# Unit-triangular 128x128 inverses by Horner's rule over block columns, and layer norms as (a - mean) * scale

## The reference

```python
x0 = layernorm(x)                       # (x - m) / sqrt(v + eps), no weights
h  = layernorm(x0) * dn_g + dn_b
q, k, v = split(h @ gates_w + gates_b, 3);  lr = h @ lr_w + lr_b
k  = k / norm(k)
A  = tril(k @ k.T, -1) + eye(512)
u  = solve_triangular(A, v, lower=True)
y  = (q @ k.T) @ (lr * u) ;  x1 = x0 + y @ out_w + out_b
x2 = x + x1 + relu((layernorm(x1) * mn_g + mn_b) @ w1 + b1) @ w2 + b2
out = x2 + (silu(n @ wg.T) * (n @ wu.T)) @ wd.T,   n = layernorm(x2)
```

## Time and profile before

| | us |
|---|---|
| Median of 3 runs (range) | 1793.11 (1792.05 to 1793.13) |
| The profiled execution, its own time | 1798.49 |
| Its span in the trace | 1796.8 |
| PE busy | 1713.0 (95%) |
| DVE busy | 1264.6 (70%) |
| POOL busy | 970.2 (54%) |
| ACT busy | 760.8 (42%) |

### The profile page before, as it was taken

How to read it: one execution, slowest core, us unless ns; L and a number is a source line. 1 busy time by engine, 2 the same in 40 slices (tenths; PEclk the granted TensorE clock), 3 DMA queues, 4 the chain that set the end, 5 groups by cost and what they waited for, 6 DMA issues and landing times.

```text
span 1796.8 us, 32849 instructions
## 1 busy us (share of the span) xinstructions
PE 1713.0 (95%) x11682; PEld 1549.5 (86%) x11682; DVE 1264.6 (70%) x2927; ACT 760.8 (42%) x1626; POOL 970.2 (54%) x1269
## 2 busy tenths in 40 slices
PE   5899999579999999999999999999999999999997
PEld 5899999478888889888888888888888899888886
DVE  4677787257777776777777777777776666676664
ACT  4668777123333333333333333333333333333432
POOL 4456775235555555555555555555555555555552
PEclk8999999689999999999999999999999999999999
DMA  4655565311111121111111211111112111111100
GB/s 124 229 194 186 200 209 181 139 40 41 52 53 52 52 76 52 54 59 56 53 53 53 76 52 52 53 52 52 52 53 64 53 51 51 51 53 59 61 16 24
DMA packets 112669, 140.83 MB, mean 78 GB/s; under 512 B 42389, under 2 KB 94872, under 8 KB 112536
## 3 DMA queue, kind: packets, MB, share of 16 engines
q1 hardware_dynamic: 112536, 139.11, 23.5%
HBM read 80.03 MB, written 59.05 MB: 77 GB/s over the span
## 4 chain that ended last, share of the span: by engine, by line
PE 62%; POOL 8%; DVE 6%; issue 4%; ACT 1%; DMA 0%; POOLq 0%; DVEq 0%; ACTq 0%
PE ps L150 29%; PE ps L1002 12%; PE ps L1012 8%; PE ps L917 5%; POOL xn L1447 5%; PE ps L933 4%; PE ps L923 3%; DVE a L1411 2%; POOL sc L1437 2%; DVE bs L1416 1%; POOL ls L1439 1%; DVE mv L1229 1%; DVE hf L1265 1%; ACT sg L1131 1%; POOL sc L1441 0%
## 5 line engine op out<-in xcount | busy, mean ns | idle before, releaser
L1490 POOL TENSOR_TENSOR hl<-hf,hh 128x512 fp32r<-128x512 f32 x128 | 172.6, 1349 | 394.0 <-ACT hh L1136 394.0
L1012 PE MATMUL ps<-wdT,hh 128*128 128x256 f32 x768 | 203.9, 303 | 1.1 <-ACT sg L1131 0.9
L1265 DVE TENSOR_TENSOR hf<-ps,sg 128x512 f32<-128x512 f32 x192 | 132.5, 690 | 88.1 <-PE ps L1002 85.1
L1012 PE MATMUL ps<-wdT,hl 128*128 128x256 f32 x768 | 187.2, 281 | 0.3 <-DVE hl L1270 0.3
L1136 ACT ACTIVATE hh<-hf 128x512 fp32r<-128x512 f32 x192 | 121.4, 632 | 155.1 <-DVE hf L1265 152.0
L1131 ACT ACTIVATE sg<-ps 128x512 f32<-128x512 f32 x192 | 113.6, 592 | 134.3 <-PE ps L1002 134.3
L1002 PE MATMUL ps<-xh3T_hi,wgT 128*128 128x512 f32 x384 | 154.7, 403 | 0.7 <-DVE xh3T_lo L1270 0.7
L1140 ACT ACTIVATE z_hi<-ps 128x256 fp32r<-128x256 f32 x128 | 49.2, 385 | 248.3 <-PE ps L933 246.6
L1002 PE MATMUL ps<-xh3T_lo,wgT 128*128 128x512 f32 x384 | 152.3, 396 | 0.0
L1002 PE MATMUL ps<-xh3T_lo,wuT 128*128 128x512 f32 x384 | 152.0, 396 | 0.0
L1002 PE MATMUL ps<-xh3T_hi,wuT 128*128 128x512 f32 x384 | 151.9, 396 | 0.0
(11 more groups left out here) (223 smaller groups left out, 5818.6 us busy)
## 6 DMA issues: line engine op xcount, KB each, us to landing
gg_scratch<-gg SPq DMA_DIRECT2D x32, 640.0 KB, 3.3
gg<-gg_scratch SPq DMA_DIRECT2D x32, 640.0 KB, 3.8
kx_scratch<-kx SPq DMA_DIRECT2D x32, 522.0 KB, 2.8
kx<-kx_scratch SPq DMA_DIRECT2D x32, 522.0 KB, 3.5
xk<-in_L_attn_x_dram SPq DMA_DIRECT2D x32, 512.0 KB, 4.1
xt<-in_L_attn_x_dram SPq DMA_DIRECT2D x32, 512.0 KB, 4.6
out_dram<-ot SPq DMA_DIRECT2D x32, 512.0 KB, 2.9
low_scratch<-gg SPq DMA_DIRECT2D x128, 16.0 KB, 1.5
```

The lines of the kernel that those rows point to most:

```text
L1012: mm = pe.matmul(ps[:, (FG, FU)[j // 2], (j % 2) * C:(j % 2 + 1) * C], part[:, h, blk(j)], wdT[:, h, :], start=(h == 0 and part is hh), st ...
L1265: dve.tensor_tensor(hf[:, h % 2, :], ps[:, up_bank(h), :], sg[:, h % 2, :], ALU.mult).then_inc(hf_ev[h], 1)
L1490: pool.tensor_tensor(hl[:, h, :], hf[:, h % 2, :], hh[:, h, :].bitcast(F32), ALU.subtract).then_inc(hl_ev[h], 1)
```

## The change

The inverse of a 128x128 block with 32x32 diagonal inverses D is built with one matrix P = -(D G), strictly block lower, and Horner's rule: X = D; X = D + P X, three times, each time on fewer block columns. PE needs the left factor transposed, which is P^T = -(G D^T) with G symmetric, so D^T is wanted too. It is made on the lanes: a new `invert_flip` copies each lane's inverse transposed, once per slot, and a second scratch `invT_scratch` and second set of four block loads bring it in as `xT32`.

- PE: no transposes of `x32`; four levels in place of five, of 96, 96, 64 and 32 columns.
- ACT: no copy of the transposed x32 (128x512); the copy of odd quarters (128x256) becomes one of the last 32 columns (128x128).
- DVE: one mask (128x384) in place of two of 128x256; additions of 128x384, 128x256 and 128x128 in place of three of 128x256; inverse steps placed otherwise among the `up` operations; three flips. POOL: one flip in the first stage.
- SP: eight block loads per sequence in place of four, at two places of its queue, and a second store and a wait per slot.
- Norms: scale only on POOL (two small operations in place of four); `xn` = (a - mean) * scale in place of a * scale + shift, on POOL and on DVE.
- The hardware loop over the last eight sequences is written out as straight code.
- Some waits on `ready` go (before `xn` on POOL, before each bn_aggr on DVE); bn_aggr of the first norm waits for the last `xn`.

```diff
+        def invert_flip(eng, lanes, m, done):
+            low, inv, subd = lanes[0], lanes[1], lanes[-1]
+            eng.wait_ge(subd, (SUB - 1) * (m + 1))
+            eng.tensor_copy(low[:, :].rearrange("p (r c) -> p r c", c=SUB),
+                            inv[:, :].rearrange("p (r c) -> p c r", c=SUB)).then_inc(done, 1)
...
-                    for i in range(NS - GROUP):
-                        body(eng, i, True, i >= 1, i >= 2, i // GROUP, i % GROUP)
-                    with eng.Fori(NS - GROUP, NS) as i:
-                        body(eng, i, True, True, True, None, None)
+                    for i in range(NS):
+                        slot, r = (i // GROUP, i % GROUP) if i < NS - GROUP else (None, None)
+                        body(eng, i, True, i >= 1, i >= 2, slot, r)
...
-                def pe_level(pe, bank, lhs, rhs, done):
+                def pe_level(pe, bank, lhs, rhs, c0, w, done):
                     for j in range(TB):
+                        mm = pe.matmul(ps[:, bank, j * w:(j + 1) * w], lhs(j), rhs[:, j, c0:c0 + w], start=True, stop=True)
...
-                        wait(pe, inv_in, i * 16 * QPB)
-                        after(pe, a0_ev[TB - 1], i)
-                        for j in range(TB):
-                            mm = pe.transpose(ps[:, A2, blk(j)], x32[:, j, :], ident[:, :])
-                        mm.then_inc(xT_ps, 1)
+                        wait(pe, inv_in, i * 32 * QPB)
                         pe.wait_ge(gg_in, (i + 1) * 16)
                         after(pe, a0_ev[1], i)
-                        pe_level(pe, A0, diag, lambda j: quarters(x32[:, j, :], 0), p32_ps)
+                        pe_level(pe, A0, diag, xT32, SUB, REST, pT_ps)
...
-                        pe_level(pe, A1, lambda j: xT32[:, j, :], lambda j: quarters(p1[:, j, :], 0), x64_ps)
-                        pe_level(pe, A2, lambda j: p1[:, j, :], lambda j: quarters(xT32[:, j, :], 1), xT64_ps)
+                        pe_level(pe, A1, p_of, x32, 0, REST, xa_ps)
...
-                        pe_level(pe, A0, diag, lambda j: x64[:, j, 0:HALF], p64_ps)
+                        pe_level(pe, A0, p_of, x64, 0, HALF, xb_ps)
...
-                        pe_level(pe, A1, lambda j: xT32[:, j, :], lambda j: p2[:, j, :], x128_ps)
+                        pe_level(pe, A1, p_of, x64, 0, SUB, x128_ps)
...
-                        act.activation(flat(xT32), ps[:, A2, :], ACT.Copy).then_inc(xT_ev, 1)
-                        act.activation(quarters4(x64, 1), quarters4(x32, 1), ACT.Copy).then_inc(x64_odd, 1)
+                        act.activation(x64[:, :, REST:P], x32[:, :, REST:P], ACT.Copy).then_inc(xd_tail, 1)
...
+                    dve.tensor_tensor(p1[:, :, SUB:P], levels(A0, REST),
+                                      upper[:, SUB:P].unsqueeze(1).broadcast_to([P, TB, REST]), ALU.mult).then_inc(pT_ev, 1)
+                    dve.tensor_tensor(x64[:, :, 0:w], levels(bank, w), x32[:, :, 0:w], ALU.add).then_inc(done, 1)
...
-                    pool.tensor_tensor(sc[:, 0, :], ls[:, 0, :], mhalf4[:, :], ALU.pow).then_inc(steps[1], 1)
-                    pool.wait_ge(steps[1], n_done)
-                    pool.tensor_tensor(ls[:, 1, :], sc[:, 0, :], mv_[:, :, 0], ALU.mult).then_inc(steps[2], 1)
-                    pool.wait_ge(steps[2], n_done)
-                    pool.tensor_tensor(sc[:, 1, :], zero4[:, :], ls[:, 1, :], ALU.subtract).then_inc(done, 1)
+                    pool.tensor_tensor(sc[:, :], ls[:, :], mhalf4[:, :], ALU.pow).then_inc(done, 1)
...
-                    pool.wait_ge(ready, 1)
                     pool.wait_ge(made, n_done)
                     for j in range(TB):
-                        op = pool.tensor_scalar(dst[:, j, :], src[:, j, :], scale[:, j:j + 1], shift[:, j:j + 1],
-                                                ALU.mult, ALU.add)
+                        op = pool.tensor_scalar(dst[:, j, :], src[:, j, :], mean[:, j, 0:1], scale[:, j:j + 1],
+                                                ALU.subtract, ALU.mult)
...
                 def load_blocks(sp, n):
-                    sp.wait_ge(x64_ev, n)
-                    sp.wait_ge(x64_odd, n)
-                    wait(sp, inv_out, 16 * (n // GROUP))
-                    load_inv(sp, n)
-                    sp.wait_ge(p64_ps, n)
+                    sp.wait_ge(pT_ps, n)
+                    wait(sp, inv_out, 32 * (n // GROUP))
+                    load_inv(sp, n, xT32, invT_v)
                     sp.wait_ge(gl_lo, n)
                     sp.dma_start(gg[:, :], gg_d[n]).then_inc(gg_in, 16)
+                    sp.wait_ge(x128_ev, n)
+                    sp.wait_ge(xd_tail, n)
+                    load_inv(sp, n, x32, inv_v)
```

More of the change, by code:

```diff
@@ L131, in delta_block_kernel @@
         x32 = sb("x32", [P, TB, P])
+        xT32 = sb("xT32", [P, TB, P])
         kx3 = kx[:, 0:KXE].rearrange("p (j c) -> p j c", j=TB)
@@ L224, in setup_pool @@
                                    base=0, pattern=[[-1, P]], channel_multiplier=1).then_inc(id_done, 1)
[L225 to L233, removed]
+                pool.memset(upper[:, :], 0.0).then_inc(zeroed, 1)
+                pool.wait_ge(zeroed, 1)
+                for a in range(QPB - 1):
+                    pool.memset(upper[a * SUB:(a + 1) * SUB, (a + 1) * SUB:P], -1.0).then_inc(minus, 1)
+                pool.wait_ge(minus, QPB - 1)
                 pool.memset(eps4[:, :], EPS)
@@ L654, in finish_sp @@
             def finish_sp(sp):
-                sp.wait_ge(inv_out, 16)
-                for a in range(QPB):
-                    sp.dma_start(x32[a * SUB:(a + 1) * SUB, :, a * SUB:(a + 1) * SUB], inv_v[0][a]).then_inc(first_in, 16)
+                sp.wait_ge(inv_out, 32)
+                for t, v in ((x32, inv_v), (xT32, invT_v)):
+                    for a in range(QPB):
+                        sp.dma_start(t[a * SUB:(a + 1) * SUB, :, a * SUB:(a + 1) * SUB], v[0][a]).then_inc(first_in, 16)
                 sp.dma_start(xt[:, :, :], x_v[0]).then_inc(first_in, 16)
@@ L1201, in _, with levels, masked, plus @@
                     overlapped(act_body)(act)
-                def masked(dve, dst, mask, src_ps, done, i):
-                    dve.wait_ge(src_ps, i + 1)
[L1206 to L1217, removed]
+                def levels(bank, w):
+                    return ps[:, bank, 0:TB * w].rearrange("p (j c) -> p j c", c=w)
+                def masked(dve, i):
+                    dve.wait_ge(pT_ps, i + 1)
+                    dve.tensor_tensor(p1[:, :, SUB:P], levels(A0, REST),
+                                      upper[:, SUB:P].unsqueeze(1).broadcast_to([P, TB, REST]), ALU.mult).then_inc(pT_ev, 1)
+                def plus(dve, bank, w, src_ps, done, i):
+                    dve.wait_ge(src_ps, i + 1)
+                    dve.tensor_tensor(x64[:, :, 0:w], levels(bank, w), x32[:, :, 0:w], ALU.add).then_inc(done, 1)
                 def dve_w(dve, i, j):
@@ L1306, in dve_invert @@
                     if r is not None:
-                        for q in range(INV_EACH * r + first, min(INV_EACH * r + end, INV_STEPS)):
-                            invert_step(dve, lanes, m, q // 2, q % 2)
+                        for q in range(INV_EACH * r + first, min(INV_EACH * r + end, INV_STEPS + 1)):
+                            if q < INV_STEPS:
+                                invert_step(dve, lanes, m, q // 2, q % 2)
+                            else:
+                                invert_flip(dve, lanes, m, flipped)
                 def dve_body(dve, i, att, mlp, down, m, r):
                     if att:
-                        masked(dve, quarters4(p1, 0), mask32[:, :].rearrange("p (q c) -> p q c", c=SUB)[:, 0::2, :]
-                               .unsqueeze(1).broadcast_to([P, TB, 2, SUB]), p32_ps, p32_ev, i)
+                        masked(dve, i)
                     if down:
@@ L1319, in dve_body @@
                         dve.tensor_copy(gl2[0][:, :], gg[:, OFF:GW]).then_inc(gl_hi, 1)
-                        plus(dve, quarters4(x64, 0), A1, quarters4(x32, 0), x64_ps, x64_ev, i)
-                        plus(dve, quarters4(xT32, 1), A2, quarters4(xT32, 1), xT64_ps, xT64_ev, i)
+                        plus(dve, A1, REST, xa_ps, xa_ev, i)
                     if mlp:
@@ L1378, in dve_body @@
                     if r == 0:
-                        wait(dve, inv_out, 16 * m)
+                        wait(dve, inv_out, 32 * m)
                         invert_start(dve, lanes, m)
@@ L1416, in dve_body @@
                             dve.bn_stats(bs2[:, j, :], a0[:, j, :]).then_inc(bn2[j], 1)
+                        after(dve, xh2_done, i)
                         dve_stats(dve, i + 1, bs2, mv2, bn2, mv2_done)
@@ L1427, in _, with pool_norm @@
                     overlapped(dve_body)(dve)
-                def pool_norm(pool, n_done, read, n_read, mv_, ls, sc, steps, mvd, done):
+                def pool_norm(pool, n_done, read, n_read, mv_, ls, sc, plus_eps, mvd, done):
                     for k in range(CB):
```

96 lines of the change are left out of this document (47 added, 49 removed).

## The result

The changed kernel takes 1861.59 us (median of 4 runs, 1856.51 to 1867.94) beside 1793.12 (4 runs, 1792.05 to 1798.36): a ratio of 1.0372, interval 1.0355 to 1.0389. It is 68 us slower; 25 us faster were forecast. The profiled execution took 1859.3 us, its span is 1856.9.

The account below looks back on a forecast made before the run. PE, busy 95% of the span, was taken to bound the kernel. 30 x (0.65 + 0.1) = 22.5, + 2 + 1.3 + 0.7 + 1.1 - 2.1 - 0.4 = 25.1 us saved: 1793.1 to 1768, range 1750 to 1782 (8 in 10).

Parts of the forecast that it names:

- POOL's part: POOL's norm chain before PE's transposes: xn starts earlier but DVE holds POOL up, so 0.65 us saved per iteration.
- Levels do not go by width: PE's inverse levels: 96 or 32 columns take 0.81 to 0.86 us each; only the number of levels counts.
- `xn` starts 1.05 to 1.15 earlier: POOL's first norm: without the two small operations, xn starts 1.05 to 1.15 us earlier.
- The block passes on to the first `xn`, the second hl to the fourth: POOL beside DVE: first xn inherits the standstill, second hl delays the fourth; PE's wait grows to 0.8 us.
- POOL not held: Rival at POOL's xn: DVE does not hold it up, 1.1 + 0.1 us per iteration, 1754 us; chance 0.22.
- the heavier collision: Rival: early xn delays hl, hf and hh; only 0.2 to 0.4 us gained per iteration, 1781 us; chance 0.15.
- The z step gains 0.1: First z step after the MLP waits for the x128 addition, which shrinks to 128 elements: about 0.1 us per iteration.
- Four more loads 2.1 us: End of the first stage: four more block loads cost 1.8 to 2.4 us once, taken as 2.1.
- A slower end only by hl losing the port: Rival: POOL's first xn takes the port ahead of hl, delaying the sixth down block; 1801.5 us, chance 0.04.
- Iterations with inverse steps, 2 us (0 to 6), periods 43.7: Iterations with inverse steps on DVE: reordering removes m_lo waits, 2 us for all together (0 to 6), periods near 43.7.
- Their hl and xn stand as in iteration 25: Iterations with inverse steps: hl and xn placed as in iteration 25, so the same 0.65 us is saved.
- the terms met once: Outside the repeated iterations: gains 1.3 and 0.7 (iterations 0, 1), 1.1 (tail); costs 2.1 (loads), 0.4 (flips).

Follow-up runs that it names:

- m1: Only POOL's tensor_scalar, 128x256 fp32 four times per form, nothing beside it: (mult, add) 0.55 us, (subtract, mult) 1.22 us.
- e3: Changed kernel with POOL's xn as (mult, add) instead of (subtract, mult), no longer computing the norm: 1763.18 us, ratio 0.9827.
- e6: Changed kernel with 20 matmuls whose results nobody uses put into PE's wait for xn: 1831.48 us, ratio 1.0199.
- run 1763: The e3 run: changed kernel with POOL's xn as (mult, add) instead of (subtract, mult), 1763.18 us.
- e1: Changed kernel with the norms of the kernel before put back on POOL and DVE: 1786.7 us, ratio 0.9956.
- e10: Changed kernel, mean negated on ACT, POOL's xn as (add, mult), POOL's addition of xt and b2 moved behind xhm_lo: 1742.24 us, ratio 0.97.
- e7: Kernel before with only its loop over the last eight sequences written out: 1795.03 us, ratio 0.9999.
- e4: Changed kernel with xn of the first norm moved from POOL to DVE, as (subtract, mult): 1789.85 us, ratio 0.9969.
- e9: Changed kernel with first norm's xn on DVE and POOL's addition of xt and b2 moved behind xhm_lo: 1731.54 us, ratio 0.9636.

## Why the prediction was wrong

**The step that failed** is the one in POOL's part: "it ends at 1445.38, the second at 1445.92, the third at 1446.46". It puts 0.55 us on each `xn`, the duration of the row of before, which is that of another pair of operations. The new pair was part of the change and got no price, no bound and no rival. m1 measured 1.22 us each. Four of them take 4.8 us alone and 5.46 in place, against a forecast of 3.4. That fills the miss: 1861.6 (changed) - 1763.2 (e3) = 98 us, where the forecast missed by 1861.6 - 1768 = 94. Of these, 30 x (2.81 - 0.66) = 65 us are the longer wait and 30 the lower clock behind it (e6).

**Point by point.**
- *Levels do not go by width*: right, 0.81 for 96 and for 32 columns, in the range of 0.81 to 0.86.
- *`xn` starts 1.05 to 1.15 earlier*: right, 1.60 - 0.48 = 1.12.
- *The block passes on to the first `xn`, the second hl to the fourth*: the changed kernel hides it; e3 shows it. Wait 0.66 (forecast 0.8), period 42.84 (42.8), `xn` done 3.78 us into the iteration (3.91), the run 1763 (1768). `xn` is done 1.30 - 0.66 = 0.64 us sooner in e3 than in e1, with PE's own work the same; 0.65 were forecast. Of the rivals, POOL not held and the heavier collision are thereby both out.
- *The z step gains 0.1*: its distance is 1590.15 - 1589.85 = 0.30, before 0.46. The term was 0.16, and the cover that I named, the addition's size, was half the story: POOL's addition held the cast ahead of it, which e10 takes away too (periods 42.84 to 42.20).
- *Four more loads 2.1 us*: 1.86, in SP's timeline of the changed kernel:

```profile
325.52 2.37 SPq L669 DMA_DIRECT2D x<-inv_scratch  x4
327.94 1.86 SPq L669 DMA_DIRECT2D xT<-invT_scratch  x4
```

- *The loop written out is worth nothing*: right (e7).
- *A slower end only by hl losing the port*: the sign came from elsewhere. With 5.46 us of `xn`, the second hl did take 0.88 us, but it was done long before PE could use it.
- *Iterations with inverse steps, 2 us (0 to 6), periods 43.7*: too small. In the kernel before the 22 iterations from 428.01 to 1400.34 take 44.20 on average, 0.58 more than those behind them (43.62). In e3 they take 42.92 against 42.84, in e1 43.56 against 43.49. So some 11 us went here, with either norm. The step that failed is "Their hl and xn stand as in iteration 25": PE's wait for `xn` was 0.52 to 0.56 us in 11 of them, where iteration 25 has 0.24. These 0.3 and the waits for m_lo, 2.7 us, make 6 of the 11; what made the rest, and what share the new places of the steps have, is not shown.

What stays open: why POOL treats the pairs so differently, and why 23 of 30 equal waits bring the clock down and 7 do not. No run tells these apart. e3 is 5 us better than forecast, but its iterations with inverse steps alone give 9 us more than their term in the sum, so some of the terms met once must be worse than forecast; apart from the loads they were not read singly.

## What to carry to other kernels

An instruction with another pair of arithmetic operations is a new instruction: price it, even if shape, line and engine stay. On POOL (x - m) * s was faster as (x + (-m)) * s, with the negation on an engine that had room. When a wait is removed and the gain does not come, look at which long operation of POOL now stands beside a short one of DVE, and move the long one to where nothing short waits for it. Where a wait of PE can't be removed, filling it may pay for itself through the clock, as e6's 30 us did.

## What the runs showed of the hardware

- POOL's tensor_scalar with two operations has two paces, 0.83 and 3.34 ns an element, by the pair (m1). DVE makes no such difference between (subtract, mult) and (mult, add), 407 and 408 ns.
- POOL and DVE can hold each other up until an instruction has ended. A 0.43 us cast took 2.33 us behind an addition of 1024 elements (e4); an addition that reads PSUM kept its 0.42 us beside POOL (1442.55 in e4). Not every pair collides, but moving that one addition took 58 us off (e4 to e9). In the prediction I drew on the Trainium skill, "GPSIMD Engine Reference", section 8, for POOL being held by DVE. The rows of e4 show the other direction, DVE held by POOL, and at a larger price.
- At 23 of the 30 waits of 2.81 us the granted clock stood at 0.50 for some 3 us or twice that. It cost 30 us over the run (e6). The prediction had no term for it, since no wait was to grow that long.
